# A Trainium2 kernel of four chained image layers: the zero products between the first projections leave, and the first loads change queues

## What is computed

```python
theta = (einsum('bhwc,cd->bhwd', x, w_theta) + b_theta).reshape(b, loc, c8)          # loc = 256, c8 = 16
phi = maxpool2x2(einsum('bhwc,cd->bhwd', x, w_phi) + b_phi).reshape(b, down, c8)     # down = 64
g = maxpool2x2(einsum('bhwc,cd->bhwd', x, w_g) + b_g).reshape(b, down, c2)           # c2 = 64
attn = softmax(einsum('bnd,bmd->bnm', theta, phi), axis=-1)
attn_g = einsum('bnm,bmd->bnd', attn, g).reshape(b, h, w, c2)
return x + (einsum('bhwd,dc->bhwc', attn_g, w_o) + b_o) * sigma
```

## Time and profile before

| | |
|---|---|
| median of 3 runs | 165.41 us (164.75 to 165.59) |
| profiled execution, its own time | 165.08 us |
| its span (first to last instruction) | 163.2 us |
| TensorE busy (matmuls) | 156.6 us, 96% of the span |
| ScalarE, VectorE, GpSimd busy | 111.2, 103.0, 54.0 us |
| bytes read from HBM, written | 4.01 MB, 1.05 MB |

### The profile page before, as it was taken

One profiled execution on the slowest core, in us unless ns is written; L12 is line 12 of the kernel. 1 busy time (PEld: TensorE's weight loads), 2 busy tenths in 40 slices (PEclk: granted clock), 3 DMA queues, 4 the chain that ended last, 5 costly groups with the idle time before them and its releaser, 6 DMA issues.

```text
span 163.2 us, 3882 instructions
## 1 busy us (share of the span) xinstructions
PE 156.6 (96%) x1477; PEld 119.8 (73%) x1477; DVE 103.0 (63%) x257; ACT 111.2 (68%) x261; POOL 54.0 (33%) x129
## 2 busy tenths in 40 slices
PE   6999999999999999999999999999998999999992
PEld 4778888988777866587686698667955766659892
DVE  0454798788899897388763595378578653115443
ACT  3395667897774488736789668756785758885870
POOL 7475696595432441105223212410210000007300
PEclk9999999999999999999999999999999999999999
DMA  4895000000000000000000001000000011000003
GB/s 143 244 375 221 4 4 0 0 6 0 0 0 4 4 1 7 0 4 4 0 0 6 0 7 35 0 4 4 21 15 4 6 34 36 4 0 0 0 4 129
DMA packets 3233, 5.43 MB, mean 33 GB/s; under 512 B 400, under 2 KB 2320, under 8 KB 3216
## 3 DMA queue, kind: packets, MB, share of 16 engines
q1 hardware_dynamic: 2928, 4.99, 9.0%
q10 hardware_dynamic: 288, 0.21, 0.4%
HBM read 4.01 MB, written 1.05 MB: 31 GB/s over the span
## 4 chain that ended last, share of the span: by engine, by line
PE 82%; DVE 8%; ACT 4%; POOL 2%; DMA 2%; issue 1%; DVEq 0%; POOLq 0%
PE psum L690 9%; PE psum L669 9%; PE psum L701 9%; PE psum L617 4%; PE psum L597 4%; DVE nmax L1183 3%; PE psum L462 3%; PE psum L645 3%; ACT pT L957 3%; PE psum L771 2%; PE psum L712 2%; PE psum L523 2%; PE psum L763 2%; PE psum L588 2%; PE psum L742 2%; PE psum L728 2%
## 5 line engine op out<-in xcount | busy, mean ns | idle before, releaser
L1183 DVE TENSOR_REDUCE nmax<-psum 128x4 f32<-128x1024 f32 x32 | 38.0, 1217 | 17.9 <-PE psum L669 17.9
L957 ACT ACTIVATE pT<-psum 128x1024 f32<-128x1024 f32 x32 | 31.6, 1025 | 10.6 <-PE psum L690 10.6
L669 PE MATMUL psum<-qk 32*128 32x256 f32 (+1 forms) x256 | 18.2, 398 | 0.1
L690 PE MATMUL psum<-qk 17*128 17x256 f32 (+1 forms) x256 | 18.2, 398 | 0.0
L701 PE MATMUL psum<-pT,vaug_all 128*32 128x256 f32 x256 | 16.9, 385 | 0.0
L358 POOL TENSOR_TENSOR rstd<-vare,half 128x1 f32<-128x1 f32 x16 | 8.9, 558 | 22.3 <-DVE vare L1142 22.0
L669 PEld LDWEIGHTS psum<-qk 32*128 32x128 f32 (+1 forms) x256 | 11.7, 184 | 5.0 <-issue 2.3
L690 PEld LDWEIGHTS psum<-qk 17*128 17x128 f32 (+1 forms) x256 | 11.7, 184 | 4.0 <-issue 1.9
L364 POOL COPY zE<-zE 128x17 f32<-128x17 f32 x8 | 1.6, 199 | 35.1 <-ACT zE L973 35.1
L701 PEld LDWEIGHTS psum<-pT,vaug_all 128*32 128x32 f32 x256 | 6.9, 109 | 6.0 <-issue 2.5
L462 PE MATMUL psum<-busy 128*128 128x256 bf16 x51 | 9.3, 320 | 1.2 <-POOL busy L318 1.1
(11 more groups left out here) (165 smaller groups left out, 364.0 us busy)
## 6 DMA issues: line engine op xcount, KB each, us to landing
out<-x SPq DMA_DIRECT2D x8, 128.0 KB, 1.9
tab<-in_weights SPq DMA_DIRECT2D x1, 644.0 KB, 9.4
tab<-in_weights SPq DMA_DIRECT2D x1, 640.0 KB, 5.0
x0T<-in_xT SPq DMA_DIRECT2D x4, 128.0 KB, 3.2
xin<-in_x SPq DMA_DIRECT2D x2, 256.0 KB, 7.2
x0T<-in_xT_rest SPq DMA_DIRECT2D x1, 512.0 KB, 7.5
xin<-in_x SPq DMA_DIRECT2D x1, 512.0 KB, 8.3
tab<-in_weights SPq DMA_DIRECT2D x1, 384.0 KB, 8.6
```

The lines of the kernel that those rows point to most:

```text
L669: last = mm(bank[(b0, b1)[j // 2] + j % 2][:, u * TOK:(u + 1) * TOK], at[:, u, 0, :], at[:, :, 1, :], start=True, stop=True)
L690: last = mm(bank[(b0, b1)[j // 2] + j % 2][:, m * TOK:(m + 1) * TOK], at[:, m, 1, :], at[:, :, 0, :], start=True, stop=True)
L957: go(pT[g](i)[:, 2 * k:2 * k + 2].rearrange("p j m t -> p j (m t)"), pair(home["st", g, i][k]), ACT.Exp).then_inc(s["exp" + "EO"[g]], 1)
L1183: v.tensor_reduce(nmax2(i)[:, g, 2 * k:2 * k + 2, :], pair(home["sm", g, i][k]).rearrange("p j (u m) -> p j u m", u=TILES), AX.X, ALU.max, ...
```

## The change

The zero products between `proj0(0)` and `proj0(1)` (8) and between `proj0(1)` and `gwm(0)` (2) are left out. `busy` is set by VectorE as its first instruction and has a semaphore of its own, `zeros`, for which TensorE and ScalarE wait instead of `filled`. `load_x` moves out of SP's block so that both queues can use it: image 1 becomes the first load of ACT's queue, where `tab0` stood, and `tab0` becomes the second of SP's, where image 1 stood.

```diff
@@ -254,6 +254,10 @@
+        def load_x(issue, i):
+
+            issue(x0T(i), xT[i]).then_inc(s[f"x0T{i}"], 16)
+
...
@@ -292,7 +292,10 @@
-            load_x(0); load_x(1); load_x(2); load_x(3)
+            load_x(sp.dma_start, 0)
+            load_table(sp.dma_start, 0)
+            load_x(sp.dma_start, 2)
+            load_x(sp.dma_start, 3)
             load_table(sp.dma_start, 2)
             load_tokens(0, 2)
             load_rest()
@@ -315,8 +318,7 @@
             def fill():
-                gp.memset(busy[:, :], 0.0).then_inc(s["filled"], 1)
-                gp.memset(half[:, :], -0.5)
+                gp.memset(half[:, :], -0.5).then_inc(s["filled"], 1)
                 gp.memset(theta_all[:, :, :], 0.0)
                 gp.memset(gw_all[:, :, :, :], 0.0).then_inc(s["filled"], 1)
@@ -781,8 +783,8 @@
-            pe.wait_ge(s["filled"], 1)
-            keep_clock(9, 7); proj0(0, 0); keep_clock(8, 7); proj0(1, 1); keep_clock(2, 7); gwm(0, 2)
+            pe.wait_ge(s["zeros"], 1)
+            keep_clock(9, 7); proj0(0, 0); proj0(1, 1); gwm(0, 2)
@@ -838,9 +840,9 @@
-            load_table(nc.scalar.dma_start, 0)
+            load_x(nc.scalar.dma_start, 1)
             load_table(nc.scalar.dma_start, 1)
-            act.wait_ge(s["filled"], 1)
+            act.wait_ge(s["zeros"], 1)
             go(warm[:, :], busy[:, 0:1], ACT.Exp)
@@ -1030,6 +1032,8 @@
             v = nc.vector
+
+            v.memset(busy[:, :], 0.0).then_inc(s["zeros"], 1)
```

More of the change, by code:

```diff
@@ L241, in build @@
         produced = """tab0 tab1 tab2 tab3 tab4 x0T0 x0T1 x0T2 x0T3 x0T4 xin0 xin2 xin4
-            filled w0s w1n fold_b b_rd wide_b fold_vo w1_rd vo_rd halves mlp_ab fold_in fold1_rd fold2t_rd fold2_rd c_rd w2n fold_b2 b2_rd wide_b2 fold_o2 o2_rd
+            zeros filled w0s w1n fold_b b_rd wide_b fold_vo w1_rd vo_rd halves mlp_ab fold_in fold1_rd fold2t_rd fold2_rd c_rd w2n fold_b2 b2_rd wide_b2 fold_o2 o2_rd
             proj0 pooled theta phi pg gw_ps s0 nmax0 gw p0 p0T_ps p0T o0 inv0 x1 x1T xT1 x1b
@@ L272, in _ @@
         def _(sp):
-            def load_x(i):
-                sp.dma_start(x0T(i), xT[i]).then_inc(s[f"x0T{i}"], 16)
             def load_rest():
```

## The result

The changed kernel's median is 165.81 us over 21 runs (165.08 to 166.55, and one of 375.96 that the comparison leaves out, as it does one run each of `w_z` and `w_before` further down, 168.52 and 167.32), against 165.43 us for the kernel before in the same jobs (164.75 to 165.78). The ratio is 1.0026, 95% interval 1.0013 to 1.0038: slower by 0.4 us. The profiled execution took 166.15 us.

What follows compares the result with a forecast made beforehand. TensorE, working in order, waits at proj0(4) for images 4 to 7. Arrival 0.55 us sooner, 0.4 lost there, net -0.1 to -0.2: 164.9 against the profiled 165.08; median 0.33 higher, less 0.3 for late executions: 165.1 us, range 164.5 to 165.9.

Steps and rivals of the forecast that it cites:

- Zeros by VectorE ... Worth 0.: Fill of the zeros moved to VectorE: TensorE begins 0 to 0.3 us sooner but waits for tab0 all the same; worth 0.
- would gain more of the 0.5: Executions reaching proj0(4) late, by a later clock rise, gain more of 0.5 us; 0.3 taken off the median for it.
- The clock: Rival at TensorE's start: clock stays low for longer without the zero products; 166.0 to 168 us, chance 0.10.
- The sum: TensorE's arrival at proj0(4): -1.84 + 0.79 + about 0.2 + 0.3 = -0.55 us, net -0.1 to -0.2.
- The rival's formula, t/2 + 4.58 + 2.35: TensorE's arrival at proj0(4) if the clock rises at t; decides from t = 9.9, where the loss is 0.8 us.
- The wall: proj0(4) waits for images 4 to 7, landing at 11.02; 0.4 us of gain lost there; 164.8 to 165.4, chance 0.60.
- That the load might move by itself with the exchange: Load of images 4 to 7 may land a little sooner, SP's queue carrying 54.5 KB less before it; 0.1 us taken.
- the thin stretch from 3.75 to 4.00: Slack in the DMA engines when ACT's loads were done, share 0.27; given as support for an earlier load of images 4 to 7.
- tab0: Second in SP's queue, lands at 3.7, proj0(0) 0.3 us later; rival that it lands at 4.37: 165.2 to 165.8, chance 0.13.
- Image 1 on ACT's queue, tab1: Image 1 lands by 3.6, wanted at about 4.7; tab1 gets 0.13 us of extra bytes with 0.3 us of room; free.

Runs made afterwards that it cites:

- w_z: Kernel before without the 10 zero products and with the load of images 4 to 7 ahead of the tokens of images 0 and 1: 165.18 us, ratio 0.9995.
- w_before: Kernel before with only the load of images 4 to 7 moved ahead of the tokens of images 0 and 1: 165.07 us, ratio 0.9979.
- m_only: Kernel before with the fill of the zeros on VectorE alone: 165.79 us, ratio 1.0026.
- pad_start: Kernel before with one spare memset at the start of VectorE's list, fill still on GpSimd: 165.72 us, ratio 1.0020.
- pad_end: Kernel before with one spare memset at the end of VectorE's list: 165.34 us, ratio 0.9993.
- pad2_start: Kernel before with two spare memsets at the start of VectorE's list: 165.34 us, ratio 0.9990.
- after_pad: Changed kernel with one spare memset behind VectorE's fill of the zeros: 165.44 us, ratio 0.9999 to the kernel before.
- qz: Changed kernel with GpSimd's fill of the zeros as before: 165.53 us, ratio 1.0010 to the kernel before.
- z_only: Kernel before with the 8 and 2 zero products left out alone: 165.33 us, ratio 1.0009.
- w_zfill: Kernel before with 10, 0 and 3 zero products and the load of images 4 to 7 ahead of the tokens: 164.81 us, ratio 0.9966.
- zfill: Kernel before with 10 zero products ahead of proj0(0), none between projections, 3 ahead of gwm(0), loads as before: 165.39 us, ratio 0.9997.
- front13: Changed kernel with 13 zero products ahead of proj0(0) instead of 9: 165.96 us, ratio 1.0043 to the kernel before.
- q_only: Kernel before with the two loads exchanged alone (tab0 second on SP, image 1 first on ACT): 166.0 us, ratio 1.0037.
- zm: Changed kernel with the loads in the queues of before: 165.73 us, ratio 1.0023 to the kernel before.
- nofront: Changed kernel without the 9 zero products ahead of proj0(0): 166.03 us, ratio 1.0052 to the kernel before.

## Why the prediction was wrong

**The step that failed: "Zeros by VectorE ... Worth 0."** The fill itself is free, as the prediction had it: VectorE needs 0.17 us for it and TensorE began at 1.04 instead of 1.08. But the step counted the instruction only where it runs, and not as a place in VectorE's list. The shift by one costs 0.37 us near 85 us in every trace that has it and in none that has not; `m_only`, `pad_start`, `pad_end`, `pad2_start` and `after_pad` show that it is the shift. Without it the changed kernel is at 165.53 (`qz`) or 165.44 (`after_pad`), which can't be told from before. So this one term is nearly all of the loss of 0.4 us.

**The gain: a second step that failed.** The 165.1 lay 0.3 us under the median of before. Some 0.1 to 0.2 of it was to come from the load of images 4 to 7, and the rest from executions that reach the wall late, which "would gain more of the 0.5". In the traces they gain nothing: where the clock rises late the real products run at half pace, and `proj0(4)` started at 11.54 in `z_only` and at 12.14 in the changed kernel, against 11.21. Without the shift by one the products left out are worth nothing that the runs can tell: ratios 1.0009 (`z_only`), 1.0010 (`qz`), 0.9999 (`after_pad`).

**The clock: a term mis-sized, and a rival underrated.** The sum had the clock rise where it rose before, about 6.1 us. In the changed kernel's trace it rose at about 10.1, with TensorE idle 0.90 us ahead of `proj0(0)` and 0.23 ahead of `gwm(0)`. The rival's formula, t/2 + 4.58 + 2.35, gives 12.0 for t = 10.1, and `proj0(4)` started at 12.14. The closeness is in part luck: the formula has TensorE at its second projection at 4.7, and it came there at about 5.05 and stood another 0.23 us. With both put in it gives 12.3, so the price holds within 0.2 us. The start was 0.93 us late, which is past the 0.8 from which the rival was to decide; behind `proj0(4)` 0.69 were left. A chance of 0.10 was too low for such a rise, though the median of the changed kernel stayed under the rival's 166.0 to 168.

When the clock rose, each from the one trace of a kernel:

| TensorE's holes (0.15 us or more) before the rise | rise at about |
|---|---|
| none (`pad_end`, `w_zfill`, `zfill`) | 4.2, 6.0, 6.1 us |
| 0.24 to 0.34 us ahead of `proj0(0)` (before, `pad_start`, `pad2_start`, `m_only`, `front13`) | 4.5 to 6.1 us |
| 0.64 us ahead of `proj0(0)` (`q_only`) | 7.5 us |
| 0.29 to 0.90 ahead of `proj0(0)` and 0.23 ahead of `gwm(0)` (changed, `z_only`, `qz`, `zm`, `w_z`, `after_pad`) | 7.4 to 10.4 us |
| idle until 4.0, then 0.23 ahead of `gwm(0)` (`nofront`) | 10.6 us |

`zfill` and `w_zfill` have no products between the projections either and rose at 6, so it goes with the holes and not with the products as such. The holes do not fix the time: `z_only` and `w_z` have the same TensorE list and the same holes, and rose at 9.5 and 7.5. How often each kernel rises late is not shown by one trace.

**The wall: right where TensorE reaches it early, but not the reason for the result.** `front13`, `zfill`, `m_only` and others show the wait for images 4 to 7 by name (0.7 to 1.25 us of idleness in them), and moving the load frees it. The reading that the kernel before stood there already is borne out: its `proj0(4)` started 0.14 us after the landing (11.07, 11.21), as in the traces that name the wait. In the changed kernel's own trace `proj0(4)` came about 1 us behind the landing and did not wait, and `w_z`, with the wall out of the way, gained nothing clear of noise. The forecast took 0.5 us of gain up to the wall and lost 0.4 of it there; in the traces with a late clock there was no such gain to lose. That the load might move by itself with the exchange (0.1 us of gain were taken) is not shown: it landed at 10.98 to 11.85 with the queues exchanged and at 10.2 to 11.5 without. Nor was the thin stretch from 3.75 to 4.00 a time in which ACT's loads were done: `tab1`, issued at 1.14 and landed 2.9 us later, was still on its way.

**tab0: right, its loss a little larger than taken.** It landed at 3.99 (3.7 was taken, the range reached to 4.37), and over the six traces with the loads exchanged at 3.70 to 4.29, against 3.19 to 3.49 in the others. The middles are 3.89 and 3.38, so the price is about the one issue slot of 0.45 us that the prediction gave, with more in single executions. Beside all the zero products the exchange costs 0.6 us (`q_only`); with the 10 left out nothing of it can be told (`qz` has 1.0010 and `z_only` 1.0009).

**Image 1 on ACT's queue, tab1:** free, as forecast, in the changed kernel's trace. VectorE's scaling began at 4.38, long before `pooled(0)` at 5.30, and `proj0(1)` followed `proj0(0)` at once.

Open is what makes the stall. The trace has no record of what VectorE's stream waits for. In the records the second of the two waits of `x3` stands directly ahead of the operation, and in the traces shifted by one the 0.4 us lie between those two, while one instruction earlier or later the same pause would fall under an operation that runs for 0.4 us. This is argued from the order of the records. A pause at a fixed place of the list, for new instructions to come in, would explain the traces with the pause and those without. The Trainium skill (Runtime: NRT & Kernel Launch, "Instruction fetch mechanics") says that an engine's instructions come in blocks and that crossing a boundary is mostly hidden. If the pause is such a crossing, it was hidden in the lists shifted by none and by two, and cost 0.4 us in those shifted by one. That it is one was only argued, and no run here shows it.

## What to carry to other kernels

Products that keep the clock up should fill the holes in which the engine waits anyway, and not stand between operations that could run; in the traces with a late rise, leaving them out gave the time back at half pace. Before counting what a shorter list gains, look for the next load that the list has to meet: here it stood 0.1 us behind, and behind it stood the next (`tab3`). And one instruction more at the head of a list can cost 0.4 us at a place far behind it, so an unexplained step between two traces is found by aligning them, and tested with a spare instruction at the start and at the end.

## What the runs showed of the hardware that was not expected

- A VectorE list shifted by one instruction shows 0.40 us of "issue" ahead of one operation at 85 us; shifted by two or by none it does not. Worth 0.2% of this kernel.
- The same load of 512 KB, issued at 3.5 us behind the same bytes in the two queues together, landed 6.7 to 8.3 us after its issue, each time in one execution of another kernel. Where TensorE waited for it, `proj0(4)` started 0.14 us after the landing (the kernel before, `front13`, `m_only`, `pad_start`).
- The rise of TensorE's clock to 2.4 GHz came anywhere from 4.2 to 10.4 us in kernels that began their products at about 1 us, and at 10.6 in one that began at 4.0. It came by 6.1 us in the traces with no hole or one of at most 0.34 us before the rise, and at 7.4 us or later in those with one of 0.64 us or with two. Two executions with the same TensorE list and the same holes rose 2 us apart.
